# Attention of two layers: output products of two key tiles together, 96-row maxima in three banks, the row of maxima by DMA

## The chip, the cores and the metric

The kernel runs on one core of a Trainium2 chip. The metric is the time of one execution in microseconds (us) on the device. TensorE is called PE, its weight loads PEld, VectorE DVE, ScalarE ACT, GpSimd POOL, SyncE SP.

## The reference

The input is a map of 32 x 32 positions with 384 channels, taken as 1024 tokens. Three parts follow each other.

```python
x = x + conv_attention(group_norm(x))     # layer 0
t = tokens(x)
t = t + attention(layer_norm(t))          # layer 1
t = t + moe(layer_norm(t))                # 8 experts, the best 2 of each token
```

Each attention has 12 heads of 32 columns over the 1024 tokens:

```python
scores = scale * q @ k.T                  # layer 0: + rel_h + rel_w, looked up per row and column
out = softmax(scores, axis=-1) @ v
out = out @ proj_w.T + proj_b
```

In layer 0 the relative positions are added to the scores through a table for rows and one for columns of the map.

## The kernel before, in words

All three parts are one program with hand-written queues for each engine, held together by counting semaphores. `for L in L2` runs each engine through the two attention layers, and the experts follow.

**A layer.** Queries, keys and values are computed (lines 562 and 650). Queries and keys are split into a high and a low part of float32r and stored in DRAM as `heads`, from where SP loads each head's operands: `load_m` (line 366) `qm` and `km` for the maxima, `load_a` (line 374) `qa`, `ka` and in layer 0 `qb` for the scores. Two sets of buffers alternate. `store` (line 385) puts a finished head's quarter rows into `xnT`.

**Maxima.** The softmax needs the maximum of each query's row before the exponential. `max_scores` (line 569) computes, for a tile of 128 queries and a half of the keys, rough scores of the high parts alone in a PSUM bank, in layer 0 with 96 rows (the relative positions too), in layer 1 with 32. The halves alternate between banks 0 and 1. DVE's `maximum` (line 857) reduces each bank of 128 x 512 to a column of `mhalf`, and after the eighth tile `mhalf` to `mcol` (line 864). Head h + 1's last three tiles are treated in steps 0 to 2 of head h, and head h + 2's first five in steps 3 to 7 (`MAXIMA`).

**From a column to a row.** The scores are computed transposed, keys on partitions and queries along the row. So the maxima, one for each query, must become a row. PE transposes `mcol` into bank 7 (`turn_max`, line 578) and ACT copies it in eight pieces into rows 96 to 103 of `qa`, each time with another column of a negated unit matrix (`place_max`, line 1051). Rows 96 to 103 of `ka` are ones, and so the score product subtracts the maximum: it has 104 rows.

**A head.** PE's `head` (line 620) goes through eight key tiles s. Each step has `scores` of tile s (two halves, in layer 0 two products for each, banks 2 to 5 in two pairs), the two maxima products, and `out_product` of tile s - 2 (`BEHIND`). An output product is four `quarters` (line 596): values 128 x 32 are the weights, 256 queries move, and each quarter goes to its own 32 columns of the array and 32 partitions of bank 6. Each fp32 quarter is two records in the trace, so a block of quarters reads "x8". ACT makes the exponential of a tile of 128 x 1024 from two banks into one of five buffers of `prob` (`NP`). The sums of the exponentials come from POOL, which adds the first tiles (`ADDS`: tiles 0 to 5 in layer 0, 0 to 4 in layer 1) into `acc`, and from PE, which multiplies the rest and `acc` with ones (`sums`, line 616). ACT copies both halves of bank 6 to `vsb`, DVE inverts the sums in four pieces (line 870) and multiplies (line 875) into `osb`. DVE also adds the bias of the projection to `t` (line 900) before the last head.

PE's queue fixes the order of its work. A product waits for the buffers and banks that it names; what stands behind it waits too. SP's queue is as strict: `load_m(h + 1)`, `load_a(h)`, in layer 1 three fills with zeros that the experts need, `store(h - 2)`.

## Time and profile before

| | us |
|---|---|
| median of three runs | 1052.12 |
| lowest and highest run | 1039.26, 1052.98 |
| span of the profiled execution | 1051.4 |
| PE busy | 943.1 (90%) |
| DVE busy | 539.0 (51%) |
| ACT busy | 421.2 (40%) |
| POOL busy | 307.3 (29%) |
| heads of layer 0 | from about 122 to 347 |
| heads of layer 1 | from about 431 to 652 |

The profile describes one execution and gives its span, from the first to the last instruction. Its own time is not listed apart from the runs; the span stands 0.7 us below their median. In a row of the timeline stand the start and the duration, engine, line, operation, what is written and read, the count where equal instructions follow each other, and in brackets the idle time before and what ended it. PE's products are pipelined, so a duration is longer than the distance to the next product, and starts are what counts.

### The profile page before, as it was taken

The numbers are of one execution on the slowest core, as the hardware profiler recorded it, in microseconds if no ns is written. First come the engines' busy times: TensorE is split into PE (matmuls) and PEld (weight loads), VectorE is DVE, ScalarE is ACT, GpSimd is POOL, SyncE is SP. The second block draws the span as 40 slices with busy tenths as digits, with TensorE's granted clock in tenths as the row PEclk, the third lists the DMA queues.
The fourth block names the chain that finished last, engine by engine and source line by source line (L and its number), as shares of the span: only waits on it lengthen the run. The fifth ranks groups of instructions, "written<-read, shape, count | busy, mean of one in ns | idle before, by whom it ended". The sixth has DMA issues, their size and how long they took to land.

```text
span 1051.4 us, 17622 instructions
## 1 busy us (share of the span) xinstructions
PE 943.1 (90%) x6029; PEld 625.0 (59%) x6030; DVE 539.0 (51%) x903; ACT 421.2 (40%) x774; POOL 307.3 (29%) x168
## 2 busy tenths in 40 slices
PE   4968899999999899999999999814999999999992
PEld 3456455555554444433444444514999999999992
DVE  4324667676774535534777775560244334433424
ACT  0211265665656222434666766221334323422420
POOL 0000175765758100333565647032000000000203
PEclk9989699999999999756999999856999999999997
DMA  8556523424334039113364556062256246345214
GB/s 280 113 127 175 226 71 98 129 78 120 103 84 147 5 68 233 30 41 106 116 202 127 187 150 207 27 229 79 74 189 232 94 164 229 130 165 192 75 52 135
DMA packets 73951, 139.03 MB, mean 132 GB/s; under 512 B 10800, under 2 KB 48688, under 8 KB 73904
## 3 DMA queue, kind: packets, MB, share of 16 engines
q1 hardware_dynamic: 62736, 120.42, 37.6%
q10 hardware_dynamic: 9120, 11.74, 3.4%
q0 software_dynamic: 2048, 6.29, 1.9%
q8 instruction: 24, 0.39, 0.2%
q14 instruction: 23, 0.19, 0.1%
HBM read 91.29 MB, written 43.45 MB: 128 GB/s over the span
## 4 chain that ended last, share of the span: by engine, by line
PE 72%; DVE 8%; issue 7%; POOL 7%; DMA 3%; ACT 2%; ACTq 1%; SPq 1%; DVEq 0%; POOLq 0%
PE ps L601 13%; PE ps L575 11%; PE ps L591 11%; PE ps L776 10%; PE ps L765 9%; PE ps L562 6%; PE ps L593 4%; POOL qf L501 3%; PE ps L696 2%; PE ps L650 2%; PE ps L672 2%; POOL xs L526 2%; POOL gy L533 2%; DVE w_lo L980 1%; DVE mhalf L860 1%
## 5 line engine op out<-in xcount | busy, mean ns | idle before, releaser
L860 DVE TENSOR_REDUCE mhalf<-ps 128x1 f32<-128x512 f32 x384 | 248.1, 686 | 142.9 <-PE ps L575 138.9
L1043 ACT ACTIVATE prob<-ps 128x1024 f32<-128x1024 f32 x192 | 196.5, 1024 | 146.0 <-PE ps L593 75.3
L501 POOL TENSOR_TENSOR qf<-qf,prob 128x1024 f32<-128x1024 f32 x84 | 205.5, 2447 | 22.3 <-POOL qf L501 9.6
L591 PE MATMUL ps<-qa,ka 104*128 104x512 f32 x384 | 164.4, 470 | 3.6 <-ACT qa L1056 2.9
L765 PE MATMUL ps<-xT,w 128*128 128x128 f32 x1440 | 165.6, 277 | 1.4 <-ACT xT L1114 1.4
L765 PEld LDWEIGHTS ps<-xT,w 128*128 128x128 f32 x1440 | 165.0, 193 | 1.8 <-issue 1.8
L575 PE MATMUL ps<-km,qm 96*128 96x512 f32 (+1 forms) x384 | 150.3, 466 | 4.8 <-DVE mhalf L860 2.8
L601 PE MATMUL ps<-prob,va 128*32 128x256 f32 x1536 | 129.5, 411 | 0.3 <-issue 0.2
L1136 ACT ACTIVATE h_f<-ps,b1c 128x128 f32<-128x128 f32 x240 | 66.9, 378 | 148.8 <-PE ps L765 148.8
L591 PEld LDWEIGHTS ps<-qa,ka 104*128 104x128 f32 x384 | 68.6, 200 | 83.0 <-issue 59.5
L575 PEld LDWEIGHTS ps<-km,qm 96*128 96x128 f32 (+1 forms) x384 | 70.1, 201 | 69.6 <-DVE mhalf L860 42.0
L497 POOL TENSOR_TENSOR qf<-prob 128x1024 f32<-128x1024 f32 x24 | 57.0, 2376 | 163.7 <-ACT prob L1043 163.7
L776 PE MATMUL ps<-w_hi,h_hi 128*128 128x384 f32 x240 | 82.1, 342 | 9.9 <-DVE h_lo L989 9.9
L533 POOL DMA_INDIRECT gy<-low,where_i x8 | 10.0, 1254 | 272.9 <-SPq L471 270.7
L776 PE MATMUL ps<-w_lo,h_hi 128*128 128x384 f32 x240 | 80.4, 335 | 0.0
L776 PE MATMUL ps<-w_hi,h_lo 128*128 128x384 f32 x240 | 80.3, 335 | 0.0
L987 DVE CAST h_hi<-h_f 128x512 fp32r<-128x512 f32 x60 | 25.5, 425 | 103.8 <-ACT h_f L1136 103.8
L593 PE MATMUL ps<-qb,eb 128*128 128x512 f32 x192 | 77.3, 403 | 0.0
L601 PEld LDWEIGHTS ps<-prob,va 128*32 128x32 f32 x1536 | 31.4, 110 | 73.0 <-issue 60.2
L1056 ACT ACTIVATE qa<-ps,negd 8x128 fp32r<-8x128 f32 x192 | 57.7, 349 | 38.4 <-PE ps L581 35.8
L562 PE MATMUL ps<-xnT,wqkv 128*128 128x512 f32 x144 | 64.1, 607 | 3.1 <-DVE xnT L821 3.1
L511 POOL COPY va<-vf 128x256 f32 (+1 forms) x24 | 9.6, 398 | 192.7 <-DVE vf L846 103.3
(129 smaller groups left out, 914.6 us busy)
## 6 DMA issues: line engine op xcount, KB each, us to landing
w<-in_w SPq DMA_DIRECT2D x24, 768.0 KB, 7.4
w_raw<-in_w SPq DMA_DIRECT2D x24, 768.0 KB, 11.9
heads<-parts SPq DMA_DIRECT2D x56, 256.0 KB, 4.6
qa<-heads SPq DMA_DIRECT2D x24, 256.0 KB, 3.8
ka<-heads SPq DMA_DIRECT2D x24, 256.0 KB, 4.3
qb<-heads SPq DMA_DIRECT2D x12, 512.0 KB, 5.3
xs<-zero SPq DMA_DIRECT2D x8, 768.0 KB, 4.9
qm<-heads SPq DMA_DIRECT2D x12, 384.0 KB, 3.7
```

Source lines behind the costliest of these rows:

```text
L501: pool.tensor_tensor(acc[b], acc[b], prob[:, n % NP, :], ALU.add).then_inc(a_ok[L], 1)
L562: last = mm(ps[:, 2 * (u % 2) + half, :], wqkv[:, k, col * P:(col + 1) * P], xnT[:, k, half * HALF:(half + 1) * HALF], start=(k == 0), sto ...
L575: mm(ps[:, half, :], qm[b][0:kr, qt * P:(qt + 1) * P], km[b][0:kr, half * HALF:(half + 1) * HALF], start=True, stop=True).then_inc(sm_ok[L ...
L591: last = mm(out, ka[b][:, s * P:(s + 1) * P], qa[b][:, cols], start=True, stop=(L == 1))
L593: last = mm(out, eb[:, s * P:(s + 1) * P], qb[b][:, cols], start=False, stop=True)
L601: last = mm(ps[HD * r:HD * (r + 1), 6, half * QUARTER:(half + 1) * QUARTER], lhs, src[:, r * QUARTER:(r + 1) * QUARTER], start=start, stop ...
L765: last = mm(ps[:, g, c % HG * P:(c % HG + 1) * P], w1[b][:, k, c * P:(c + 1) * P], xT[:, k, :], start=(k == 0), stop=(k == KT - 1))
L776: last = mm(ps[:, 6, 0:C], h[:, c, :], w[:, c, :], start=(c == 0 and n == 0), stop=(c == HC - 1 and n == 2))
L860: v.tensor_reduce(mhalf[:, b, qt, half:half + 1], ps[:, half, :], AX.X, ALU.max).then_inc(mx_ok[L], 1)
L1043: act.activation(prob[:, s % NP, :], ps[:, 2 + 2 * (s % 2):4 + 2 * (s % 2), :].rearrange("p a b -> p (a b)"), ACT.Exp).then_inc(p_ok[L], 1)
L1056: last = act.activation(qa[b][96:104, i * P:(i + 1) * P], ps[0:TT, 7, 0:P], ACT.Copy, scale=negd[:, i:i + 1])
L1136: last = act.activation(h_f[:, c, :], ps[:, g, c % HG * P:(c % HG + 1) * P], ACT.Relu, bias=b1c[b][:, c:c + 1])
```

## The change

- Order: `head` on PE goes through pairs of key tiles: scores and maxima of both, then the output products of the two tiles of the pair before.
- Maxima: three banks (0 to 2) in a ring written out in `MAX_BANK` and `MAX_BACK`; the scores move to banks 3 to 6, the output to bank 7. The products have 96 rows in layer 1 too; POOL writes zeros into rows 32 to 95 of `qm` once. The tile of queries is now every eighth query (`qt:N:TT`), so that `mcol` read row by row is in the order of the queries.
- Row of maxima: no transposition and no copies by ACT. SP writes `mcol` to DRAM and reads it back as one row into row 96 of `qa` (`load_row`); row 96 of `ka` is -1. The score product has 97 rows.
- POOL multiplies by the inverted sums (`multiply`), after its additions of the next head, and adds the bias of the projection at the layer's start.
- `prob` has six buffers, and in the last head POOL adds only tiles 0 to 2.
- SP's order in the loop is `load_a`, `load_row`, `load_m`, fills, `store`.

```diff
-NP = 5
+NP = 6
...
-BEHIND = 2
 ADDS = (5, 4)
+ADDS_LAST = 2
+MAX_BANK = (0, 1, 2, 0, 1, 2, 0, 1, 2, 0, 1, 2, 0, 1, 2, 1)
+MAX_BACK = (4, 2, 4, 3, 3, 3, 3, 3, 3, 3, 3, 3, 3, 3, 3, 2)
+OUT_BANK = 7
...
+        row_dram = [nc.dram_tensor(f"row{b}", [N], F32).ap() for b in range(2)]
...
+        bd = vsb[:].rearrange("p a b -> p (a b)")[:, 0:2 * REL * 4].rearrange("p (w i g) -> p w i g", w=2, g=4)
...
+                def load_row(h, b):
+                    sp.wait_ge(mc_ok[L], h + 1)
+                    sp.sem_inc(m_free, 1)
+                    sp.dma_start(row_dram[b].rearrange("(p t) -> p t", t=TT), f(mcol[:, b, :])).then_inc(st_row, 16)
+                    wait(sp, st_ok[L], TT * (h - 1))
+                    sp.sem_inc(m_free, 1)
+                    sp.wait_ge(st_row, 16 * (L * NH + 1) + 16 * h)
+                    sp.sem_inc(m_free, 1)
+                    sp.dma_start(f(qa[b][96:97, :]), row_dram[b].unsqueeze(0)).then_inc(ld_row[b], 16)
...
+                load_row(0, 0)
                 load_m(2, 0)
-                load_a(2, 0)
+                load_row(1, 1)
                 load_m(3, 1)
-                store(0, 0, 0)
                 with sp.Fori(0, (NH - 4) // 4) as q:
                     for n in range(4):
-                        h = q * 4 + n + 3
-                        load_m(h + 1, n % 2)
-                        load_a(h, 1 - n % 2)
+                        h = q * 4 + n + 1
+                        load_a(h + 1, n % 2)
+                        load_row(h + 1, n % 2)
...
+                        load_m(h + 3, n % 2)
...
-                        store(h - 2, 1 - n % 2, n + 1, q)
+                        store(h - 1, n % 2, n, q)
+                load_a(NH - 2, 0)
+                load_row(NH - 2, 0)
+                store(NH - 4, 0, NH - 4)
                 load_a(NH - 1, 1)
+                load_row(NH - 1, 1)
...
-                def add_tiles(h, b, last=False):
-                    for n in range(1, ADDS[L] + 1):
+                def add_tiles(h, b, first=False, last=False):
+                    adds = ADDS_LAST if last else ADDS[L]
...
+                    if not first:
+                        multiply(h - 1, 1 - b)
+                def multiply(h, b):
+                    wait(pool, st_o[L][b], 32 * (h - b))
+                    pool.wait_ge(o_rc[L], 4 * (h + 1))
+                    pool.sem_inc(pool_in, 1)
+                    pool.tensor_tensor(osb[b][:], vsb[:, 0, :], rec[:], ALU.mult).then_inc(o_ok[L], 1)
...
+                if L == 0:
+                    pool.wait_ge(ld_c, 16 * 16)
+                    pool.wait_ge(ld_t, 16)
+                else:
+                    pool.wait_ge(sm_ok[0], 2 * TT * NH)
+                    pool.wait_ge(o_ok[0], NH)
+                    pool.sem_inc(pool_in, 1)
+                    for i in L2:
+                        for g in (1, 2):
+                            pool.memset(f(qm[i][g * HD:(g + 1) * HD, :]), 0.0).then_inc(qm_zero, 1)
+                    pool.wait_ge(tn_ok[0], TT)
+                    pool.wait_ge(qm_zero, 4)
+                    pool.sem_inc(pool_in, 1)
+                pool.tensor_tensor(t[:], t[:], bproj[:, L:L + 1, :].broadcast_to([P, TT, C]), ALU.add).then_inc(biased, 1)
                 take_v(0, 0)
-                add_tiles(0, 0)
+                add_tiles(0, 0, first=True)
...
-                kr = 96 if L == 0 else 32
+                kr = 96
                 def max_scores(h, b, qt):
                     if qt == 0:
                         pe.wait_ge(ld_m[L][b], (h - b) * 8 * n_m + 16 * n_m)
                     for half in range(2):
-                        wait(pe, mx_ok[L], 2 * (TT * h + qt) + half - 1)
-                        mm(ps[:, half, :], qm[b][0:kr, qt * P:(qt + 1) * P],
+                        i = 2 * qt + half
+                        wait(pe, mx_ok[L], 2 * TT * h + i - MAX_BACK[i] + 1)
+                        mm(ps[:, MAX_BANK[i], :], qm[b][0:kr, qt:N:TT],
...
                 def scores(h, b, s):
                     if s == 0:
                         pe.wait_ge(ld_a[L][b], (h - b) * 8 * n_a + 16 * n_a)
-                        pe.wait_ge(r_ok[L], h + 1)
+                        pe.wait_ge(ld_row[b], 8 * (h - b) + 8 * L * NH + 16)
                     wait(pe, p_ok[L], TT * h + s - 1)
                     for half in range(2):
-                        out = ps[:, 2 + 2 * (s % 2) + half, :]
+                        out = ps[:, 3 + 2 * (s % 2) + half, :]
                         cols = slice(half * HALF, (half + 1) * HALF)
-                        last = mm(out, ka[b][:, s * P:(s + 1) * P], qa[b][:, cols], start=True, stop=(L == 1))
+                        last = mm(out, ka[b][0:97, s * P:(s + 1) * P], qa[b][0:97, cols], start=True, stop=(L == 1))
...
+                    adds = ADDS[L] if left else ADDS_LAST
+                    for pair in range(TT // 2):
+                        for s in (2 * pair, 2 * pair + 1):
+                            scores(h, b, s)
+                            for later, qt in (MAXIMA_FIRST if first else MAXIMA)[s]:
+                                if left >= later:
+                                    max_scores(h + later, b if later == 2 else 1 - b, qt)
+                        if pair > 0:
+                            for s in (2 * pair - 2, 2 * pair - 1):
+                                out_product(h, b, s, adds)
                         elif not first:
-                            out_product(h - 1, 1 - b, TT + s - BEHIND)
-                        if s == BEHIND - 1 and not first:
-                            sums(h - 1, 1 - b)
-                        if s == TT - AHEAD and left >= 1:
-                            turn_max(h + 1, 1 - b)
+                            for s in (TT - 2, TT - 1):
+                                out_product(h - 1, 1 - b, s, ADDS[L])
+                            sums(h - 1, 1 - b, ADDS[L])
...
-            own(v.memset(bd[:], 0.0))
+            own(v.memset(vsb[:], 0.0))
             for i in L2:
-                v.memset(f(ka[i][96:104, :]), 1.0)
+                v.memset(f(ka[i][96:97, :]), -1.0)
...
-                        v.wait_ge(sm_ok[L], 2 * (TT * h + qt) + half + 1)
-                        v.tensor_reduce(mhalf[:, b, qt, half:half + 1], ps[:, half, :], AX.X, ALU.max).then_inc(mx_ok[L], 1)
+                        i = 2 * qt + half
+                        v.wait_ge(sm_ok[L], 2 * TT * h + i + 1)
+                        v.tensor_reduce(mhalf[:, b, qt, half:half + 1], ps[:, MAX_BANK[i], :], AX.X, ALU.max).then_inc(mx_ok[L], 1)
...
-                        if s == 6 and not first:
-                            output(h - 1, 1 - b)
...
-                if L == 0:
-                    v.wait_ge(ld_t, 16)
-                v.tensor_tensor(t[:], t[:], bproj[:, L:L + 1, :].broadcast_to([P, TT, C]), ALU.add).then_inc(biased, 1)
...
-                        act.activation(prob[:, s % NP, :], ps[:, 2 + 2 * (s % 2):4 + 2 * (s % 2), :].rearrange("p a b -> p (a b)"),
+                        act.activation(prob[:, s % NP, :], ps[:, 3 + 2 * (s % 2):5 + 2 * (s % 2), :].rearrange("p a b -> p (a b)"),
                                        ACT.Exp).then_inc(p_ok[L], 1)
-                        if TT - AHEAD <= s < TT - 1 and not last:
-                            i = s - TT + AHEAD
-                            place_max(h + 1, 1 - b, range(PLACED[i], PLACED[i + 1]))
-                        if s == BEHIND - 1 and not first:
+                        if s == 1 and not first:
                             keep_output(h - 1)
-                def place_max(h, b, tiles):
-                    act.wait_ge(mT_ok[L], h + 1)
-                    wait(act, st_ok[L], TT * (h - 1))
-                    for i in tiles:
-                        last = act.activation(qa[b][96:104, i * P:(i + 1) * P], ps[0:TT, 7, 0:P], ACT.Copy, scale=negd[:, i:i + 1])
-                    if i == TT - 1:
-                        last.then_inc(r_ok[L], 1)
```

The order of PE's instructions in the loop of layer 1, from the third key tile of a head on, was this (va is the head's values, km and qm the operands of the maxima, an ISA or REGISTER row a wait's value).

```order
L591 MATMUL ps<-qa_57,ka_59 128x512 x2
L283 ISA
L575 MATMUL ps<-km_64,qm_62 128x512 x2
L601 MATMUL ps<-prob,va_67 32x256 x4
L283 REGISTER_ALU
L591 MATMUL ps<-qa_57,ka_59 128x512 x2
L572 ISA
L283 REGISTER_ALU
L575 MATMUL ps<-km_63,qm_61 128x512 x2
L601 MATMUL ps<-prob,va_67 32x256 x4
```

Now the same place reads:

```order
L630 MATMUL ps<-qa_57,ka_59 128x512 x2
L286 REGISTER_ALU
L619 MATMUL ps<-km_64,qm_62 128x512
L286 REGISTER_ALU
L619 MATMUL ps<-km_64,qm_62 128x512
L286 REGISTER_ALU
L630 MATMUL ps<-qa_57,ka_59 128x512 x2
L615 ISA
L286 ISA
L619 MATMUL ps<-km_63,qm_61 128x512 x2
L640 MATMUL ps<-prob,va_67 32x256 x8
```

A tile's output product stood behind each maxima pair; now two score and maxima blocks stand together and x8 is two output products.

SP's queue at the start of the loop of layer 1 began with the loads for the maxima (qm, km) and went on to those for the scores (qa, ka).

```order
L371 DMA qm_61<-heads 32x1024
L372 ISA
L372 DMA km_63<-heads 32x1024
L283 ISA
L378 ISA
L378 DMA qa_58<-heads 64x1024
L379 ISA
L379 DMA qa_58<-heads 32x1024
L380 ISA
L380 DMA ka_60<-heads 32x1024
L381 DMA ka_60<-heads 64x1024
```

Now it begins with the loads for the scores, and the row of maxima goes out and comes back before the next load.

```order
L381 DMA qa_57<-heads 64x1024
L382 ISA
L382 DMA qa_57<-heads 32x1024
L383 ISA
L383 DMA ka_59<-heads 32x1024
L384 DMA ka_59<-heads 64x1024
L390 REGISTER_ALU
L392 DMA row<-mcol 128x8
L395 ISA
L397 DMA qa_57<-row 1x1024
L286 REGISTER_ALU
L374 ISA
```

The loads for the maxima moved behind the row, and everything behind `row<-mcol` waits for DVE's `mcol` and for the row's way to DRAM.

## Rows read from the trace of the kernel before

**Rows 1.** TensorE's granted clock in 40 slices of the span, in tenths.

```profile
PEclk9989699999999999756999999856999999999997
```

**Rows 2.** Window of layer 1: us, busy us of PE, PEld, DVE, ACT, POOL, PEclk, DMA.

```profile
435.00:484.00 49.00, 48.94 (x207) 18.01 (x207) 20.74 (x36) 19.40 (x31) 19.16 (x10) 0.50 0.10 24
```

**Rows 3.** Timeline of DVE, first and last `mcol` of heads between which the pace is read.

```profile
148.79 0.17 DVE L864 TENSOR_REDUCE mcol<-mhalf 128x8 f32<-128x16 f32 x1
...
318.98 0.17 DVE L864 TENSOR_REDUCE mcol<-mhalf 128x8 f32<-128x16 f32 x1
...
436.54 0.17 DVE L864 TENSOR_REDUCE mcol<-mhalf 128x8 f32<-128x16 f32 x1
...
495.86 0.17 DVE L864 TENSOR_REDUCE mcol<-mhalf 128x8 f32<-128x16 f32 x1
...
630.66 0.17 DVE L864 TENSOR_REDUCE mcol<-mhalf 128x8 f32<-128x16 f32 x1
```

**Rows 4.** Timeline of PE in layer 0, a head's start and a later key tile.

```profile
201.97 0.61 PE L601 MATMUL ps<-prob,ones 128*32 128x256 f32 x8
...
202.41 0.61 PE L601 MATMUL ps<-qf,ones 128*32 128x256 f32 x8
...
211.65 0.50 PE L591 MATMUL ps<-qa,ka 104*128 104x512 f32 x1
...
212.70 0.62 PE L575 MATMUL ps<-km,qm 96*128 96x512 f32 x2
...
213.24 0.64 PE L601 MATMUL ps<-prob,va 128*32 128x256 f32 x8
...
213.81 0.50 PE L591 MATMUL ps<-qa,ka 104*128 104x512 f32 x1
```

**Rows 5.** Timeline of PE and DVE in layer 1, one key tile at full clock.

```profile
566.38 0.73 PE L591 MATMUL ps<-qa,ka 104*128 104x512 f32 x2
...
566.88 0.54 DVE L870 RECIPROCAL rec<-vsb 128x64 f32<-128x64 f32 x1
...
567.04 0.73 PE L575 MATMUL ps<-km,qm 32*128 32x512 f32 x2
...
567.58 1.29 DVE L860 TENSOR_REDUCE mhalf<-ps 128x1 f32<-128x512 f32 x2
...
567.70 0.64 PE L601 MATMUL ps<-prob,va 128*32 128x256 f32 x8
...
568.26 0.73 PE L591 MATMUL ps<-qa,ka 104*128 104x512 f32 x2
```

**Rows 6.** Timeline of PE, products of 96 columns, moving operand contiguous, then strided.

```profile
58.46 3.71 PE L672 MATMUL ps<-qf,bd 128*128 128x96 f32 x32
...
81.70 6.17 PE L672 MATMUL ps<-qf,bd 128*128 128x96 f32 x36
```

**Rows 7.** Timeline of SP and PE at the first head of layer 0.

```profile
119.53 0.34 SPq L371 DMA_DIRECT2D qm<-heads  x1
...
121.75 0.77 PE L591 MATMUL ps<-qa,ka 104*128 104x512 f32 x1 [2.29 <-ACT qa L1056]
```

**Rows 8.** DMA issues of the page: count, KB each, us to landing.

```profile
ka<-heads SPq DMA_DIRECT2D x24, 256.0 KB, 4.3
...
xnT<-osb SPq DMA_DIRECT2D x92, 32.0 KB, 1.8
```

**Rows 9.** Timeline: PE and POOL in a head, DVE's multiplication, POOL and PE near layer 0's end.

```profile
323.93 5.27 POOL L501 TENSOR_TENSOR qf<-qf,prob 128x1024 f32<-128x1024 f32 x1 [0.18 <-POOL qf L501]
...
346.66 0.64 PE L601 MATMUL ps<-qf,ones 128*32 128x256 f32 x8 [1.36 <-POOL qf L501]
...
555.62 0.73 PE L591 MATMUL ps<-qa,ka 104*128 104x512 f32 x2
...
560.14 2.36 POOL L497 TENSOR_TENSOR qf<-prob 128x1024 f32<-128x1024 f32 x1 [6.29 <-ACT prob L1043]
...
571.24 0.42 DVE L875 TENSOR_TENSOR osb<-vsb,rec 128x256 f32<-128x256 f32 x1
```

More of the change, by code:

```diff
@@ L336, in _ @@
             sp.dma_start(bqk[:], a["bqk"]).then_inc(ld_bq, 16)
-            for dst, name in ((ebf, "eb"), (ident[:], "ident"), (negd[:], "negd"), (before[:], "before")):
+            for dst, name in ((ebf, "eb"), (ident[:], "ident"), (before[:], "before")):
                 sp.dma_start(dst, a[name]).then_inc(ld_c, 16)
@@ L688, in _ @@
                 head(NH - 1, 1, left=0)
-                for s in range(TT - BEHIND, TT):
-                    out_product(NH - 1, 1, s)
-                sums(NH - 1, 1)
+                for s in (TT - 2, TT - 1):
+                    out_product(NH - 1, 1, s, ADDS_LAST)
+                sums(NH - 1, 1, ADDS_LAST)
                 def project(tt, ks):
```

48 lines of the change are left out of this document (16 added, 32 removed).

## The prediction

> **What bounds the kernel now.** The granted clock in 40 slices [rows 1] comes first: TensorE (PE) has full clock almost throughout, with a hole of about 58 us in the second layer's attention. The window from 435 to 484 us [rows 2] shows PE busy for the whole of it at 0.50, that is at 1.2 instead of 2.4 GHz; the same code goes on behind it at 1.00. The start of the small reduction mcol, which runs once a head at its third key tile, gives the pace [rows 3]. Layer 0: (318.98 - 148.79) / 9 = 18.91 us a head. Layer 1 at full clock: (630.66 - 495.86) / 8 = 16.85. Its two heads before that: (495.86 - 436.54) / 2 = 29.66. So the half clock costs 2 x 12.8 = 25.6 us.
>
> Inside a head the timeline shows PE issuing nearly without a break. A key tile of layer 0 takes 213.81 - 211.65 = 2.16 us [rows 4]: four score products up to 212.70 (1.05), two maxima products to 213.24 (0.54), four output quarters to 213.81 (0.57). At a head's start such blocks of quarters follow each other 202.41 - 201.97 = 0.44 apart [rows 4]. A lone block thus costs 0.13 more than one in a row, and the 512-column products around it lose some more: six at about 0.235 are 1.41, the row shows 1.59. Changing between full products and 32-column ones therefore costs 0.13 + 0.18 = 0.31 us a time, and it happens at each of 8 tiles a head.
>
> Layer 1 has two score products and two maxima products a tile, but takes 568.26 - 566.38 = 1.88 us [rows 5], against 4 x 0.235 + 0.44 + 0.31 = 1.69 by the same pieces. The rest is the pair of maxima, 0.66 instead of 0.47: with two banks each product waits for the reduction of the one two before. VectorE is nearly full there, 1.29 for two reductions and 0.54 for a reciprocal [rows 5], and a two-bank ring gives it no lead. PE bounds both layers, VectorE stands just behind in layer 1.
>
> **The change, part by part.** *Pairs.* The change takes 4 of 8 such transitions out of each head: 4 x 0.31 = 1.24 us. A head of layer 0 has 48 products of 512 columns (11.3 us), 11 blocks of quarters (8 of values, 2 of late sums, 1 of the accumulated sum: 4.84) and 4 transitions (1.24): 17.4, and I take 17.5. Layer 1 has 32 products (7.5), 12 blocks (5.3) and 1.24: 14.1.
>
> *What the pairs delay.* The last two output products of a head come behind two score tiles of the next, and with six buffers the first exponential needs the buffer of the seventh tile. In layer 1 that puts exp 0 at 2.1 + 0.9 = 3.1 us from the head's start and its end at 4.2, and PE wants the bank at 4.4. Exp 1 ends at 5.2, PE wants it at 5.35. Hidden, with 0.1 to 0.2 us to spare. In layer 0 exp 0 ends at 5.15 and PE wants it at 5.36. If the cover fails, up to 0.3 us a head is lost, 7 us in all.
>
> *Three banks.* They let a maxima product start while two reductions are outstanding, so the 0.19 a tile in layer 1 goes (8 x 0.19 = 1.5 a head). Late next is VectorE: in the third pair it has four reductions and two reciprocals, about 3.6 us, against PE's 3.1. The bank of the third product behind then stalls PE some 0.5 us. I take 14.7 us for a head of layer 1, between 14.1 (no stall) and 15.6 (0.5 in each of three pairs). VectorE also loses the multiplication of 0.42 [rows 9].
>
> *Steady sum.* Layer 0: 9 heads x (18.91 - 17.5) = -12.7. Layer 1 at full clock: 8 x (16.85 - 14.7) = -17.2.
>
> *Clock.* With 32-row maxima layer 1 had fallen to half clock by 435 us, in its first head, and stayed at 0.50 while PE was busy for all of 49 us [rows 2]; layer 0, whose maxima have 96 rows, keeps full clock once it has it [rows 1]. The change gives layer 1 the 96 rows (two thirds of them zeros on one side). If that keeps the clock, the two slow heads become ordinary: 59.32 - 2 x 14.7 = -29.9, 25.6 of it the clock's and 4.3 the steady gain. If it does nothing, these heads scale as 2 x (14.1 to 14.7), nearly the 29.66 they take, and only about -2 remains. Both ends stay in the range; I take the first, since the one difference between the layers' products that bears on it is removed, and because the clock also held at 32 rows once it was back, so the loss looks marginal. The Trainium skill, "TensorE: Matmul & The Clock Gate" (What's actually happening), says that the gate follows how busy PE has been. Read as time busy this speaks against the gain: PE was 48.94 us busy in 49 at half clock [rows 2], and rows would change nothing; the sum would be the second end. The trace already disagrees with so plain a reading.
>
> *Row of maxima by DMA.* The transposition (one product) and eight ScalarE copies a head go; ScalarE was not the bound, worth 0.1 a head. In their place SP sends 128 x 8 values out and one row of 1024 back, each a transfer at least as long as the smallest here, 1.8 us [rows 8], or as the 4.3 of a load that it queues behind. At the first head of layer 0 the store can only be issued behind the last head stores, where before a load went out at 119.53 [rows 7]; so the row lands at 119.53 + 0.5 + 2 + 0.5 + 2 = 124.5 or a little less, against scores that began at 121.75: +2.3 (bounds +1.5 to +7). At layer 1's first head I add 0.5. In the steady state SP's queue has store of outputs, then load_a, then the row, and stands first behind GpSimd's multiplication, below.
>
> *GpSimd.* Its additions begin at 560.14, when the head's score products began at 555.62 [rows 9]; with exp 1 a microsecond later they begin at 5.4, four additions of 2.36 with gaps and a copy take 11.1, and the multiplication of a quarter of their columns 0.6 to 1.1: it ends 17.5 us from the head's start. Then 2.6 to issue four stores, 2.4 for load_a, 3 to 4 until the row is out (behind loads of 4.3), 2.6 until it is back: 28.1 to 29.1 us, due within two heads, 29.4. The cover is thin: each further microsecond costs half a microsecond a head. In layer 0 it is five additions (multiplication done at 20.4), 2.6, 2.9, 5 and 2.6: 33.5 in 35.0. The bias additions (3072 columns, about three of these, 7 us) lie at the layers' starts, where GpSimd is idle. VectorE's own goes, beside which one GpSimd addition took 5.27 instead of 2.36 at 323.93 [rows 9]; half of those 2.9 us reached PE, as I estimate: -1.5. At the very end of each layer the multiplication moves from 0.42 to about 0.7 on the path: +0.3 twice.
>
> *Two additions in the last head.* PE waited 1.36 us at 346.66 for the last addition [rows 9]. That and the transitions of the last two heads (2 x 1.24) give -3.8 in layer 0, less three more blocks of ones (1.3): -2.5. In layer 1, with two blocks (0.9) and a shorter wait, about -2.0.
>
> *Strided weights.* The maxima's stationary operand is now read with steps of eight values. The only strided fp32 read in the trace is a moving one: 32 products of 96 columns take 3.71 us contiguous (0.116 each), 36 strided 6.17 (0.171) [rows 6]. If a weight load slows as much it takes about 0.2 and hides under a 0.235 product. Bounds: 0 to 0.2 us for each of 384 products, 0 to 77 us; I take 0.01, +4, near the row. "SBUF — State Buffer" of the Trainium skill (The DMA port swizzle) states that fp32 is read at full rate only within 16-byte lines; a step of 32 bytes leaves each, so it expects the slowdown, without a size. The row agrees in kind; the sum would stand, since the size is the row's.
>
> *Sum.* -12.7 - 17.2 - 29.9 - 2.5 - 2.0 - 1.5 + 2.3 + 0.5 + 0.6 + 4 = -58.4, and about -1 for the first heads before their marks: -59.4. The profiled execution's span of 1051.4 gives 992.0. It stands 0.7 under the median of the runs, 1052.12, so 993. The lowest run, 1039.26, shows that something of 13 us varies; half of the clock's 25.6 would be that size.
>
> **Rivals.** *A, the clock stays low in layer 1:* the time is 993 + 26 = 1019. For it: PE was busy and stayed low. Against: layer 0's behaviour.
> *B, the row comes late:* if each of its transfers takes 3 us more (behind the 1.5 MB of zero fills or the loads), the loops are 35 and 39.5 us, the heads 17.5 and 19.75: +2.8 x 10 and +2.25 x 10, about 1044 with the clock kept. Against: 1.8 us for small transfers, and the fills are issued after the row.
> *C, slower:* the strided weight load does not hide. Its place is each of the 384 maxima products; it decides from (59.4 + 4) / 384 = 0.16 us more each, a load of about 0.4 us. At 0.2 it gives 993 - 4 + 77 = 1066. For it: the reads of [rows 6] did slow down. Against: only by half.
> *D, the pairs gain nothing* because the cost of a transition sits elsewhere: the 12.7 of layer 0 and 8 x 1.24 = 9.9 of layer 1 vanish, 1016. The 0.44 and 0.57 of [rows 4] speak against.
>
> **How the numbers follow.** Forecast 0.62, A 0.18, B 0.08, C 0.04, D 0.08. The range reaches from 978 (14.1 us a head in layer 1, a free strided read) over A and D to 1028. A measurement of this kernel can tell about 2% from no change, 21 us. Faster by over 2% is the forecast, A, D and half of B, 0.92; same 0.04; slower 0.04, C.
>
> **What would show it.** Right: mcol every 17.5 us in layer 0 and 14.7 in layer 1; granted clock 1.0 through layer 1; maxima products 0.235 apart; two blocks of quarters 0.44 apart and one transition per pair; 4 exponentials in 8 waiting for PE alone. Wrong: PE's score products waiting for the row's DMA, maxima products waiting for VectorE in each pair, 0.50 around 430 to 490, or weight loads of the maxima over 0.23 us.

## The result and the profile after

The changed kernel takes 997.8 us (median of four runs, 992.37 to 999.31); the kernel before, on the same chip, 1052.4 (four runs, 1039.26 to 1052.98). The ratio is 0.9486, with an interval of 0.9428 to 0.9544: faster, 5 us above the forecast of 993 and inside its range. The profiled execution took 997.88, with a span of 996.1 against 1051.4. The kernel before varies much more than the changed one: in 27 later executions it took 1029.91 to 1070.83 us, with a mean granted clock from 0.910 to 0.948. The ratios use only the executions of a kernel within 1.5% of its quickest (fast ones), which leaves out slow ones of before, so they can stand nearer to 1 than the medians do.

Cut at the first score product of each layer (rows L591 before, L630 after) and at the first product of the projection, the 55.3 us of span come from these places:

| stretch | before | after | difference |
|---|---|---|---|
| to layer 0's first scores | 121.8 | 123.5 | +1.7 |
| attention of layer 0 | 225.4 | 209.8 | -15.6 |
| from there to layer 1's scores | 83.7 | 83.5 | -0.2 |
| attention of layer 1 | 221.0 | 181.0 | -40.0 |
| the rest | 399.5 | 398.3 | -1.2 |

The granted clock of the changed kernel in 40 slices, answering to [rows 1]:

```profile
PEclk9989699999999999999999999559999999999996
```

The hole of [rows 1] in the 17th to 19th slice is gone; the one further on lies behind the attention of layer 1 and stands in both. Two windows of layer 1 (busy us of PE, PEld, DVE, ACT, POOL, then PEclk), answering to [rows 2]:

```profile
414.00:470.00 56.00, 52.74 (x421) 34.71 (x419) 40.92 (x73) 29.09 (x32) 34.03 (x20) 1.00 0.40 119
470.00:583.00 113.00, 110.41 (x947) 71.34 (x944) 83.34 (x150) 60.86 (x67) 77.69 (x45) 1.00 0.52 158
```

PE is now a little less busy than in [rows 2] (94 and 98% of the time instead of all of it) and has the full clock throughout. The timeline of DVE, `mcol` once a head, answers to [rows 3]:

```profile
148.43 0.17 DVE L905 TENSOR_REDUCE mcol<-mhalf 128x8 fp32r<-128x16 f32 x1
...
308.49 0.17 DVE L905 TENSOR_REDUCE mcol<-mhalf 128x8 fp32r<-128x16 f32 x1
...
437.32 0.17 DVE L905 TENSOR_REDUCE mcol<-mhalf 128x8 fp32r<-128x16 f32 x1
...
562.25 0.17 DVE L905 TENSOR_REDUCE mcol<-mhalf 128x8 fp32r<-128x16 f32 x1
```

Layer 0: (308.49 - 148.43) / 9 = 17.78 us a head instead of 18.91. Layer 1: (562.25 - 437.32) / 8 = 15.62 instead of 16.85, and no head of 29.66. A pair of layer 0 on PE, answering to [rows 4]:

```profile
221.14 0.50 PE L630 MATMUL ps<-qa,ka 97*128 97x512 f32 x1
...
222.20 0.64 PE L619 MATMUL ps<-km,qm 96*128 96x512 f32 x2
222.67 0.39 PE L630 MATMUL ps<-qa,ka 97*128 97x512 f32 x1
...
225.19 0.50 PE L630 MATMUL ps<-qa,ka 97*128 97x512 f32 x1
```

The pair takes 225.19 - 221.14 = 4.05 us. Two tiles of [rows 4] took 4.32. The two maxima products stand 0.47 apart as a couple (222.20 to 222.67), so a product still takes 0.235 beside its strided weights. Layer 1, PE from the first pair of a head to the third, answering to [rows 5]:

```profile
508.37 0.74 PE L630 MATMUL ps<-qa,ka 97*128 97x512 f32 x2
...
512.98 0.74 PE L630 MATMUL ps<-qa,ka 97*128 97x512 f32 x2
...
514.52 0.40 PE L619 MATMUL ps<-km,qm 96*128 96x512 f32 x1
...
515.34 0.63 PE L619 MATMUL ps<-km,qm 96*128 96x512 f32 x1 [0.43 <-DVE mhalf L901]
...
515.90 1.07 PE L640 MATMUL ps<-prob,va 128*32 128x256 f32 x16
...
516.90 0.74 PE L630 MATMUL ps<-qa,ka 97*128 97x512 f32 x2
...
518.43 0.87 PE L619 MATMUL ps<-km,qm 96*128 96x512 f32 x2
...
519.23 1.07 PE L640 MATMUL ps<-prob,va 128*32 128x256 f32 x16
520.23 0.74 PE L630 MATMUL ps<-qa,ka 97*128 97x512 f32 x2
```

The four pairs of such a head take 4.61, 3.92, 3.33 and 3.75. Without any wait they would take 4.39, 3.07, 3.07 and 3.51 by the pieces of the prediction (0.235 for a product, 0.44 for a block of quarters, 0.31 for the change between them). The row of 515.34 shows the largest loss: one maxima product waits 0.43 us for a reduction, in ten heads of the layer. The rest is small and in every pair: the last couple of maxima products takes 518.43 to 519.23, 0.80 instead of the 0.57 that such a couple takes in layer 0 (223.62 to 224.19).

### The profile page after: what moved, and what is told of

Same layout as the page of the kernel before. It is cut to its first block, busy times and chain, and to the rows that moved or that the text cites. A ratio compares the mean times of both kernels' runs of the same rounds, so it can differ in the third digit from the quotient of the medians.

```text
span 996.1 us, 17661 instructions
## 1 busy us (share of the span) xinstructions
PE 879.5 (88%) x6045; PEld 675.1 (68%) x6046; DVE 500.9 (50%) x879; ACT 353.8 (36%) x582; POOL 322.3 (32%) x191
## 4 chain that ended last, share of the span: by engine, by line
PE 41%; issue 7%; DVE 6%; POOL 4%; DMA 4%; SPq 4%; ACT 1%; ACTq 1%; DVEq 0%; POOLq 0%
PE ps L816 11%; PE ps L805 9%; PE ps L640 6%; PE ps L630 5%; PE ps L619 5%; SPq L362 2%; PE ps L736 2%; POOL xs L569 2%; POOL gy L576 2%; DVE w_lo L1016 1%; DMA xnT<-osb 1%; PE ps L605 1%; DVE mhalf L901 1%; POOL qf L521 1%; DMA heads<-parts 1%
## 5 line engine op out<-in xcount | busy, mean ns | idle before, releaser
L1079 ACT ACTIVATE prob<-ps 128x1024 f32<-128x1024 f32 x192 | 190.4, 1026 | 219.5 <-PE ps L640 95.7
L521 POOL TENSOR_TENSOR qf<-qf,prob 128x1024 f32<-128x1024 f32 x79 | 188.2, 2383 | 16.2 <-POOL qf L521 8.6
L619 PE MATMUL ps<-km,qm 96*128 96x512 f32 x384 | 149.1, 463 | 7.8 <-DVE mhalf L901 6.8
L630 PE MATMUL ps<-qa,ka 97*128 97x512 f32 x384 | 146.8, 425 | 8.6 <-DMA qa<-row 8.6
L619 PEld LDWEIGHTS ps<-km,qm 96*128 96x128 f32 x384 | 113.3, 320 | 36.1 <-DVE mhalf L901 21.1
L640 PE MATMUL ps<-prob,va 128*32 128x256 f32 x1536 | 107.5, 385 | 0.0
L630 PEld LDWEIGHTS ps<-qa,ka 97*128 97x128 f32 x384 | 69.4, 191 | 54.5 <-issue 27.9
L911 DVE RECIPROCAL rec<-vsb 128x64 f32<-128x64 f32 x96 | 49.8, 535 | 39.0 <-ACT vsb L1087 39.0
L640 PEld LDWEIGHTS ps<-prob,va 128*32 128x32 f32 x1536 | 40.3, 109 | 41.2 <-issue 24.0
L1029 DVE TENSOR_TENSOR ysb<-ps,b2c 128x384 f32<-128x384 f32 x20 | 11.1, 557 | 90.7 <-PE ps L816 90.7
```

The source lines that it names most:

```text
L521: pool.tensor_tensor(acc[b], acc[b], prob[:, n % NP, :], ALU.add).then_inc(a_ok[L], 1)
L619: mm(ps[:, MAX_BANK[i], :], qm[b][0:kr, qt:N:TT], km[b][0:kr, half * HALF:(half + 1) * HALF], start=True, stop=True).then_inc(sm_ok[L], 1)
L630: last = mm(out, ka[b][0:97, s * P:(s + 1) * P], qa[b][0:97, cols], start=True, stop=(L == 1))
L640: last = mm(ps[HD * r:HD * (r + 1), OUT_BANK, half * QUARTER:(half + 1) * QUARTER], lhs, src[:, r * QUARTER:(r + 1) * QUARTER], start=star ...
L1079: act.activation(prob[:, s % NP, :], ps[:, 3 + 2 * (s % 2):5 + 2 * (s % 2), :].rearrange("p a b -> p (a b)"), ACT.Exp).then_inc(p_ok[L], 1)
```

## The experiments

**Rows of the maxima products.** The forecast laid the clock to the 32 rows and the 1.88-us tile to the two banks. *e1* takes the kernel before and gives it the 96 rows alone:

```diff
-                kr = 96 if L == 0 else 32
+                kr = 96
```

together with GpSimd's zeros in rows 32 to 95 of `qm` from the change.

> The kernel before with one thing of the change: the maxima products of layer 1 have 96 rows (rows 32 to 95 zeros in qm). Theory (the rows keep the clock): granted clock 1.0 through the heads of layer 1, the marks mcol of its first heads 16.9 us apart instead of 30.1 and 29.2, time 1052 - 25 = 1027. Rival (the clock depends on how long TensorE is busy, or was kept by the pairs or the banks): still about 58 us at 0.50, time 1052, the same.

It took 1013.5 us (1012.65 to 1017.82), a ratio of 0.9806 [0.968, 0.9931] to its kernel before. Between the profiled executions attention of layer 1 went from 221.0 to 184.7 us, and the span by 39.5; against the two quickest executions of before measured beside it (1029.91 and 1039.46) e1 is only 20 us faster. The granted clock by slices shows no hole at the 18th:

```profile
PEclk9979699999999999999999999658999999999996
```

And a window of its layer 1, columns as above, has PE nearly as busy as [rows 2]:

```profile
420.00:500.00 80.00, 79.12 (x591) 39.51 (x589) 63.61 (x107) 53.89 (x87) 44.98 (x24) 1.00 0.41 119
```

So with the rows alone this execution keeps its clock. The other executions agree: their mean granted clock is 0.947 to 0.954 in e1's four, and 0.910 to 0.948 in the seven of before measured beside them. The rows did something unforeseen too: heads at full clock went from 16.86 to 15.8 with two banks still, about 11 us in all, and therefore e1 is faster than the 1027 expected. The weight loads (PEld) say why. First the kernel before, the tile of [rows 5] and VectorE's reductions ahead of it:

```profile
566.37 0.30 PEld L591 LDWEIGHTS ps<-qa,ka 104*128 104x128 f32 x2 [0.41 <-issue]
567.04 0.29 PEld L575 LDWEIGHTS ps<-km,qm 32*128 32x128 f32 x2 [0.37 <-DVE mhalf L860]
```

```profile
565.68 1.29 DVE L860 TENSOR_REDUCE mhalf<-ps 128x1 f32<-128x512 f32 x2 [0.15 <-PE ps L575]
```

Then e1, the loads of one tile, and the products of the same:

```profile
560.12 0.30 PEld L601 LDWEIGHTS ps<-qa,ka 104*128 104x128 f32 x2 [0.41 <-issue]
560.47 0.48 PEld L585 LDWEIGHTS ps<-km,qm 96*128 96x128 f32 x2
```

```profile
560.12 0.74 PE L601 MATMUL ps<-qa,ka 104*128 104x512 f32 x2
560.70 0.63 PE L585 MATMUL ps<-km,qm 96*128 96x512 f32 x2
561.27 0.64 PE L611 MATMUL ps<-prob,va 128*32 128x256 f32 x8
```

With 32 rows the first load of the maxima comes 0.67 us after that of the scores and with its product (567.04 for both); with 96 rows it comes 0.35 after it, under the running score product, and the maxima product follows 0.58 after the first score product instead of 0.66. The same happens once more on the way out of the couple (0.57 instead of 0.66). A change between 104 and 32 rows thus costs about 0.09 us each time, and there are two in a tile: that was the 0.19. The brackets of the load at 567.04 name VectorE's `mhalf` as what it waited for, as the prediction thought. But the bank of this first product is that of the first of the two reductions from 565.68 on, which was over about 0.7 us earlier, and the next experiment leaves only the rows as a difference.

*e9* is e1 with `kr = 96 if L == 0 else 64`.

> The kernel before with 64 rows in layer 1's maxima (e1 had 96). Two things came with 96 rows: the clock stayed at 1.0 and a key tile took 1.70 instead of 1.89 us, because the weights of the first maxima product were loaded under the score product before it. If the tile's loss belongs to 32-row weights beside 104-row ones (another cut of the array), 64 rows may keep it or not: kept means 1.89, gone means 1.70. If the clock follows the rows used, 64 rows lie between: 0.50 for less than 58 us or not at all, time 1013 to 1035. If it needs all 96, 1040 to 1053.

It has e1's zeros and e1's wait for them. It took 1036.25 (ten runs, 1029.44 to 1053.35), a ratio of 0.9958 [0.9917, 0.9999]: about no gain. Its heads at full clock are 16.87, as in before. The weight load of its maxima on PEld is late as in before, and a window of its layer 1 has the clock partly down:

```profile
568.76 0.30 PEld L585 LDWEIGHTS ps<-km,qm 64*128 64x128 f32 x2 [0.36 <-DVE mhalf L872]
```

```profile
425.00:465.00 40.00, 39.87 (x167) 15.53 (x166) 18.68 (x31) 16.07 (x26) 12.98 (x8) 0.66 0.12 32
```

So neither the zeros nor the wait made e1's pace or its clock. The hole lasted 27.3 us here against 58.0 in the profile of before. One profile can't tell whether that is the rows or chance: the kernel before ran between 1029.9 and 1070.8, and e9's own runs spread by 24. In the cost of the change 64 rows act as 32 do. *e2* is the counter-test, the changed kernel with 32 rows in layer 1:

```diff
-                kr = 96
+                kr = 96 if L == 0 else 32
```

> The changed kernel with 32 rows again in layer 1's maxima. Theory (rows keep the clock): 0.50 comes back at the first head of layer 1 for some 50 us, time 998 + 20 to 26 = 1018 to 1024. Rival (pairs and banks keep the clock busy enough): clock stays 1.0, 998, the same.

It took 1063.97 (1051.94 to 1076.47), a ratio of 1.021 [0.9935, 1.0486]: the whole gain is gone, and 66 us over the changed kernel. The mean granted clock of its executions is 0.891 to 0.918, that of the changed kernel's 0.945 to 0.951. Its granted clock by slices, and a window of layer 1:

```profile
PEclk9989599999999999569696969855999999999996
```

```profile
425.00:450.00 25.00, 25.00 (x122) 10.30 (x121) 9.02 (x14) 5.94 (x7) 7.05 (x3) 0.50 0.16 43
```

The clock falls again and again, mostly in stretches of 17 to 27 us, while PE is busy all the time. Heads take 17.6 to 28.9 us, and about 17.6 at full clock, more than the 16.86 of before. The pairs don't help there: a pair has as many changes of row count as two single tiles.

**Pairs and banks.** *e3* goes back to single tiles in `head` and keeps the rest:

```diff
-                    for pair in range(TT // 2):
-                        for s in (2 * pair, 2 * pair + 1):
...
+                    for s in range(TT):
...
+                        if s >= 2:
+                            out_product(h, b, s - 2, adds)
```

> The changed kernel with TensorE's order of before: one output product behind each key tile. Theory (each change between full and 32-column products costs 0.31 us, four more a head): heads of layer 0 17.78 + 1.24 = 19.0 us, layer 1 15.60 + 0.6 to 1.2 (part of it lies under VectorE's waits), time 998 + 24 to 29 = 1022 to 1027. Rival (the gain of layer 0 came from the transposition and ScalarE's copies that went): heads of layer 0 17.8 to 18.0, time 998 to 1003.

It took 1010.79 (1007.79 to 1020.63), a ratio of 0.9751 [0.9638, 0.9864]. Heads of layer 0 are 18.83 again, +1.05 over 17.78; heads of layer 1 at full clock are 15.69, only +0.09 where 0.6 to 1.2 was expected. So the pairs are worth 13 us, nearly all in layer 0, and the three banks, the row by DMA and GpSimd's multiplication bring nothing there in the single order: most heads of before took 18.8 too.

The profiled execution of e3 shows one thing more, a window of its layer 1:

```profile
430.00:450.00 20.00, 20.00 (x84) 9.43 (x83) 9.75 (x17) 7.24 (x8) 9.83 (x5) 0.50 0.12 34
```

This kernel has 96 rows and was at half clock for 20.5 us all the same. In the 5 us before, PE had been busy for 3.56, with one wait of 1.44 us for the row of maxima. The changed kernel has the same wait there, 3.43 us busy in 415 to 420, and kept its clock. e3's four other executions took 1007.79 to 1010.8 with a mean granted clock of 0.949 to 0.953, against 1020.63 and 0.939 for this one. So 96 rows make the fall rarer and shorter; they don't rule it out.

*e6* keeps the pairs and has two banks:

```diff
-MAX_BANK = (0, 1, 2, 0, 1, 2, 0, 1, 2, 0, 1, 2, 0, 1, 2, 1)
-MAX_BACK = (4, 2, 4, 3, 3, 3, 3, 3, 3, 3, 3, 3, 3, 3, 3, 2)
+MAX_BANK = (0, 1, 0, 1, 0, 1, 0, 1, 0, 1, 0, 1, 0, 1, 0, 1)
+MAX_BACK = (2, 2, 2, 2, 2, 2, 2, 2, 2, 2, 2, 2, 2, 2, 2, 2)
```

> The changed kernel with its maxima in two banks in turn (bank 2 idle). Theory (with pairs four maxima products come within 1.2 us and the ring of banks holds them; each waits 0.7 us of reduction after the one two before): the second maxima block of each pair waits some 0.3 to 0.6 us, heads of layer 1 15.60 + 1 to 2 = 16.6 to 17.6, layer 0 17.78 + 0 to 0.8, time 998 + 11 to 26 = 1009 to 1024. Rival (three banks are worth nothing, as in the single order): 998, the same.

It took 1028.2 (1027.55 to 1030.47), a ratio of 0.9874 [0.979, 0.9958]. A pair of its layer 1 on PE:

```profile
503.69 0.74 PE L630 MATMUL ps<-qa,ka 97*128 97x512 f32 x2
504.27 0.65 PE L619 MATMUL ps<-km,qm 96*128 96x512 f32 x2
...
505.46 1.22 PE L619 MATMUL ps<-km,qm 96*128 96x512 f32 x2
506.61 1.07 PE L640 MATMUL ps<-prob,va 128*32 128x256 f32 x16
507.61 0.74 PE L630 MATMUL ps<-qa,ka 97*128 97x512 f32 x2
```

The second couple takes 505.46 to 506.61, 1.15 us instead of 0.80, and starts 0.24 late; a pair takes 3.92. Heads: 18.85 and 17.42, in layer 0 more than the forecast allowed. With four maxima products in quick succession the later ones wait for a whole reduction. The third bank is worth 30 us with pairs. Without it the pairs bring nothing in layer 0 (18.85) and cost 1.6 us a head in layer 1 (17.42 against 15.8 in e1, which has single tiles and two banks, but also the old way of the row). It is what the pairs need; a gain of its own in the single order is not shown.

*e4* only moves the two places where the ring of three is broken, since 16 is not a multiple of 3:

```diff
-MAX_BANK = (0, 1, 2, 0, 1, 2, 0, 1, 2, 0, 1, 2, 0, 1, 2, 1)
-MAX_BACK = (4, 2, 4, 3, 3, 3, 3, 3, 3, 3, 3, 3, 3, 3, 3, 2)
+MAX_BANK = (0, 1, 2, 0, 1, 2, 1, 0, 2, 1, 0, 2, 1, 0, 1, 2)
+MAX_BACK = (3, 3, 3, 3, 3, 3, 2, 4, 3, 3, 3, 3, 3, 3, 2, 4)
```

> The changed kernel with another table of banks: the two places where the ring of three breaks (a bank used again after one product) are the first products of the second and the fourth pair (products 14 and 6) instead of the second of tile 7 and of tile 0 (products 15 and 1). Theory (the second pair of each head, 3.92 us in layer 1 and 4.38 in layer 0, is long because product 1 waits for the reduction of product 15): layer 0 17.78 - 0.34 = 17.4, layer 1 15.60 - 0.6 = 15.0, time 998 - 10 = 988. Rival (VectorE is the bound, the wait moves to the next pair): same pace in layer 1, time 994 to 998.

It took 986.58 (982.87 to 988.04), a ratio of 0.9523 [0.9403, 0.9643]. The pair that contained the row of 515.34 is now 3.32:

```profile
502.01 0.74 PE L630 MATMUL ps<-qa,ka 97*128 97x512 f32 x2
...
503.54 0.85 PE L619 MATMUL ps<-km,qm 96*128 96x512 f32 x2
...
505.33 0.74 PE L630 MATMUL ps<-qa,ka 97*128 97x512 f32 x2
```

Heads: 17.44 (-0.34) and 15.02 (-0.60), 11 us in all with the ends of the layers. A product that may look back only two places waits for the reduction of the product two before it, which in a burst has only just begun. That is harmless where it opens a pair, right behind output products, as 6 and 14 do; in the changed kernel it was 15 and 1, the second and the last of one pair.

**Weights and transport.** *e5* reads the maxima's weights contiguously and has SP write the row one value at a time to put it in order:

```diff
-                        mm(ps[:, MAX_BANK[i], :], qm[b][0:kr, qt:N:TT],
+                        mm(ps[:, MAX_BANK[i], :], qm[b][0:kr, qt * P:(qt + 1) * P],
...
-                    sp.dma_start(row_dram[b].rearrange("(p t) -> p t", t=TT), f(mcol[:, b, :])).then_inc(st_row, 16)
+                    sp.dma_start(row_dram[b].rearrange("(t p) -> p t", p=P), f(mcol[:, b, :]), allow_slow_non_contiguous=True).then_inc(st_row, 16)
```

> The changed kernel with the maxima's weights read contiguously (a tile is 128 neighbouring queries again); so that the row still comes in order, SP writes mcol to DRAM one value at a time. Theory (the strided weight load takes 0.32 instead of 0.19 us but hides under the product before it): weight loads at 0.19, products of one pair still 0.235 to 0.245 apart, heads of layer 0 within 0.1 of 17.78 unless the row comes late. Rival (the stride costs time): spacing 0.235 against 0.245 at every one of 16 products plus the first one, heads 0.3 to 1 us shorter.

One run took 1159.47, against 1040.84 for before beside it. The group of the maxima's weight loads in the changed kernel (partitions x elements, count, busy us, mean ns, waits), then in e5:

```profile
L619 PEld LDWEIGHTS ps<-km,qm 96*128 96x128 f32 x384 | 113.3, 320 | 36.1 <-DVE mhalf L901 21.1 <-ACT prob L1057 1.1 <-issue 1.0
```

```profile
L619 PEld LDWEIGHTS ps<-km,qm 96*128 96x128 f32 x384 | 86.0, 225 | 52.8 <-DVE mhalf L901 30.5 <-ACT prob L1057 1.1 <-issue 1.1
```

And a line of e5's waits (us in total, times, longest):

```profile
PE ps L630 <- DMA qa<-row: 95.0, 18, 16.8
```

A contiguous load takes 0.19 (the mean of 225 includes stretches at half clock), a strided one 0.32. Under a running product both hide. Behind a wait for VectorE the load can't be early, and the difference shows: the pair of layer 1 that takes 3.33 in the changed kernel takes 3.18 in e5, and one of layer 0 0.02 to 0.04 less. With 44 pairs in each layer that is 44 x 0.15 + 44 x 0.04: an estimate of about 8 us for the stride, from a single profiled execution. Both forecasts were half right: the load hides in layer 0 and does not in layer 1. The last line is the other result: written value by value, the row comes late 18 times, most heads take 21 to 24 us, and at each such wait the clock falls to half, mostly for 6.8 us. The changed kernel's line of waits, and its transfers of `row`:

```profile
PE ps L630 <- DMA qa<-row: 8.6, 2, 7.1
```

```profile
DMA to landing us min/median/max: 1.5/3.1/5.3
```

Two waits in all, at the first head of each layer; 22 rows are hidden.

**The first row.** In layer 0 PE waits 7.12 us for it in the changed kernel:

```profile
120.49 0.35 SPq L392 DMA_DIRECT2D row<-mcol  x1
...
122.02 0.30 SPq L397 DMA_DIRECT2D qa<-row  x1
...
123.49 0.77 PE L630 MATMUL ps<-qa,ka 97*128 97x512 f32 x1 [7.12 <-DMA qa<-row]
```

*e7* puts `load_row(0, 0)` of both layers ahead of SP's wait for the last stores of heads, and *e8* joins that with e4's ring.

> The changed kernel with one thing moved in SP's queue: the first head's row of maxima is sent out and back before SP waits for the last head stores of the layer, not behind them. Theory (the first score product of each layer waits for that row, 7.1 us in layer 0 and 1.4 us in layer 1): layer 0 begins 2 to 5 us earlier, layer 1 1 us, time 998 - 3 to 6 = 992 to 995. Rival (the row then queues behind the stores in the DMA queue and lands no earlier): the same, 998.

> The bank table of e4 and the early row of e7 together. If both causes are what they seem and lie at different places, the gains add: 986.6 - 3 to 6 = 981 to 984, faster than both kernels. If the early row only moves the wait, 986 to 987.

e7 took 996.56 (993.54 to 997.4; ratio 0.9558 [0.9475, 0.9642]), e8 984.28 (984.06 to 985.71; ratio 0.9449 [0.9369, 0.9529]): 1 and 2 us under the kernels without it, which these runs can't tell from nothing. In e7 the row of layer 0 leaves 8.7 us sooner, but it is read back only 0.5 sooner:

```profile
111.77 0.35 SPq L392 DMA_DIRECT2D row<-mcol  x1
121.48 0.30 SPq L397 DMA_DIRECT2D qa<-row  x1
```

From one issue to the other it takes 9.7 us behind the stores of the heads, and 1.5 in the changed kernel, where SP had waited for these. *e10* (with e4's ring) issues both transfers of the first row from ScalarE:

```diff
-                load_row(0, 0)
+                if L == 1:
+                    load_row(0, 0)
...
+                if L == 0:
+                    act.wait_ge(mc_ok[0], 1)
+                    act.dma_start(row_dram[0].rearrange("(p t) -> p t", t=TT), f(mcol[:, 0, :])).then_inc(st_row, 16)
+                    act.wait_ge(st_row, 16)
+                    act.dma_start(f(qa[0][96:97, :]), row_dram[0].unsqueeze(0)).then_inc(ld_row[0], 16)
```

> e4 (the new bank table) with the first head's row of layer 0 moved by ScalarE's DMA queue instead of SP's, as soon as the column is there. Theory (the row waited behind the head stores in SP's queue, on the wire as well, and TensorE 6 to 7 us for it): the first score product at 117 to 119 instead of 122.5 us, time 986.6 - 3 to 5 = 982 to 984. Rival (the DMA engines are full with the stores, the queue does not matter): 122, 986.

It took 983.54 (981.52 to 985.87), a ratio of 0.9408 [0.9309, 0.9507].

```profile
111.35 0.35 ACTq L1096 DMA_DIRECT2D row<-mcol  x1
116.72 0.49 ACTq L1098 DMA_DIRECT2D qa<-row  x1
119.20 0.76 PE L631 MATMUL ps<-qa,ka 97*128 97x512 f32 x1 [2.42 <-DMA qa<-row]
```

In its own queue the row takes 5.4 us where e7's took 9.7, and the scores begin 3.3 us sooner than in e4. The median is 3 us below e4's 986.58, but the two sets of runs overlap. *e12* is e10 with layer 1's first row ahead of SP's wait for stores too.

> e10 with layer 1's first row too sent before SP waits for the last stores of queries and keys. Layer 1's first score product waited 1.4 us for it. If e10's gain holds, this adds about 1: 981 to 983; the best of all. If not, as e8: 984.

It took 983.17 (981.45 to 984.49), a ratio of 0.9406 [0.9309, 0.9504]: the same as e10. Its row in layer 1 leaves 1.1 us sooner than in e10 (402.83 for 403.96) and is read back 0.9 later (406.76 for 405.82). Both take 14 us less than the changed kernel and 58 less than the median of before measured beside them, 1041.47. That median stood at 1052.4 in the first measurement; the 11 us between the two are before's own variation.

**Who multiplies.** *e11* gives the multiplication back to VectorE:

```diff
-                    if not first:
-                        multiply(h - 1, 1 - b)
...
+                        if s == 6 and not first:
+                            output(h - 1, 1 - b)
```

> The changed kernel with the multiplication by the inverted sums back on VectorE (0.4 to 0.8 us a head), at the end of its seventh step. If VectorE were the bound of layer 1, heads grow by 0.4 to 0.8 (16.0 to 16.4), time 1002 to 1008. If TensorE waits only for the ring of banks, at fixed places of the pair, heads stay at 15.6 to 15.8, 998 to 1001.

It took 1010.61 (1007.36 to 1011.15), a ratio of 0.9664 [0.9563, 0.9765]. That is beyond both forecasts. Layer 0 keeps its 17.79; heads of layer 1 go from 15.60 to 16.8, and two of them to 18.5 and 18.6, in which the clock fell for 3.4 us, again with 96 rows. GpSimd, DVE and PE of its layer 1:

```profile
511.20 2.37 POOL L521 TENSOR_TENSOR qf<-qf,prob 128x1024 f32<-128x1024 f32 x1 [0.18 <-POOL qf L521]
...
511.77 2.09 DVE L914 TENSOR_TENSOR osb<-vsb,rec 128x256 f32<-128x256 f32 x1
513.78 2.47 DVE L899 TENSOR_REDUCE mhalf<-ps 128x1 f32<-128x512 f32 x4
...
549.84 0.62 PE L617 MATMUL ps<-km,qm 96*128 96x512 f32 x1 [0.79 <-DVE mhalf L899]
```

The multiplication, 0.42 in [rows 9], takes 2.09 and ends 0.29 after GpSimd's addition. In layer 0 it falls between two additions and takes 0.43 to 0.55. The reductions behind it come late, and PE waits. The Trainium skill, "SBUF — State Buffer" (SBUF: two separate sides), says that a VectorE operation with two inputs in SBUF and one of GpSimd that reads SBUF hold the same ports by turns, each for its whole length. These rows agree.

## Why the prediction was right, and where it was not

*Clock: right.* The two slow heads were to save 29.9 and saved 59.32 - 2 x 15.62 = 28.1. e1, e2 and e9 show the cause from both sides: 96 rows alone keep the clock in the kernel before and 64 don't, 32 rows alone lose it in the changed kernel. Rival A is out. (By the prediction's own clock paragraph, with only 2 us left of this term, it stood at 1021 and not at 1019.) Two limits remain. e3 and e11 lost the clock for 20.5 and twice 3.4 us with 96 rows (and e5 behind its long waits). And the 28.1 belong to the profiled execution of before with its hole of 58 us: the change saved 55 us of span against that one, while before's quickest execution, 1029.91 with a mean granted clock of 0.948, stands only 32 above the changed kernel. Of the plain reading of the Trainium skill, "TensorE: Matmul & The Clock Gate" (What's actually happening), by which time busy decides, e1's window (79.12 of 80 us at 1.00) and e2's (25.00 of 25 at 0.50) leave nothing: PE is busy all the time in both.

*Pairs: right in layer 0, given back in layer 1.* The ordinary pair of layer 0 takes 4.03 to 4.05 against 4.01 by the prediction's pieces, and e3 measures 1.05 a head of the 1.24. The head is 17.78 and not 17.5 because of the breaks of the ring, 0.34 by e4, which the prediction did not look at: -10.1 instead of -12.7. In layer 1 the 1.24 did not come: single tiles cost only 0.09 more there (e3), since the pairs run into the waits for VectorE described below; with e4's ring the pairs stand 0.67 below e3 (15.02 against 15.69). Rival D is out for layer 0.

*The step that failed inside a forecast that held* is "with two banks each product waits for the reduction of the one two before ... so the 0.19 a tile in layer 1 goes". It does go, but e1 removes it with two banks: it belonged to the 32 rows. Half of it sat in the two score products, which take 0.66 us in [rows 5] and 0.58 in e1 and wait for no bank of the maxima. The third bank was what the pairs needed (e6). With that the prediction's account of layer 1 loses its footing: it credited the banks with a gain that they don't give. Its head of 14.7 took 14.1 and one stall of 0.5 in the third pair. Measured are 14.1 + 4 x 0.24 for the last couple of every pair, in which product and strided load wait for a reduction, + 0.60 for the breaks: 15.66, against 15.62. So the term of layer 1 came to 8 x (16.85 - 15.62) = -9.9 instead of -17.2. The bound of 15.6 had been named; the value chosen below it was the error, and it was mostly made good by what follows.

*Strided weights.* +4 was taken; e5 gives about 8 by estimate, and it is part of the 0.24, not beside it. The sign that was to show it wrong, loads above 0.23, came (0.32), and still rival C is far off: a longer load costs only where nothing runs above it.

*Row of maxima: right.* First scores at 123.49 against "124.5 or a little less", +1.7 for +2.3. Layer 1's start moved by -0.2 for +0.5. In the steady state the estimate was 28.1 to 29.1 us from the start of a head to the landing. In the timeline, a head that starts at 508.37 has its additions from 514.09 (5.7, predicted 5.4) and its multiplication at 524.87 (ends at 17.2, predicted 17.5), the row leaves at 531.29 and is read back from 534.17 on, 25.8 us after the start. A transfer of the row lands 1.5 to 5.3 us behind its issue, so this one is there after 27 to 31 us, and two heads take 31.2, not 29.4: the cover is as thin as was said, and the slower heads helped it. Rival B's transport is not there, but e5 shows that its mechanism is: with it, 95 us of waits.

*GpSimd.* VectorE's bias additions went; what they gave is not separated. "+0.3 twice" never came, as the last multiplication of each layer stays on VectorE. The prediction gave the multiplication itself almost nothing, 0.42 off VectorE. That was its length in layer 1; in nine heads of layer 0 it took 1.04 to 1.73 in before. e11 shows that in the new order it is worth 13 us, since on VectorE it would lie behind an addition of GpSimd.

*The sum.* Short by 2.6 (layer 0's pace), 7.3 (layer 1's) and 1.8 (slow heads), 11.7 in all. Back come the +4 that these paces already hold, 0.6 for the multiplications, 1.3 for both first rows, and 1.7 that is left over and lies in the layers' ends and behind them: 4.1, which is 59.4 against 55.3. The forecast was near in part by luck, because errors cancelled. The range's lower end of 978 is 5 us below what the two terms named for it give, 993 - 6 - 4 = 983.

Open: why the clock of PE falls with 32 rows and hardly with 96 of which 64 are zeros, and what set it off in e3; how the hole of before is spread over its executions, of which only the mean clocks (0.910 to 0.948, and 0.926 for the profiled one with 58 us) are known; what the bias additions and six buffers bring by themselves, which was not tried.

## What to carry to other kernels

Before laying a gap between two products to the buffers behind them, compare the shapes on either side: here products of 104 and 96 rows follow each other smoothly, of 104 and 32 or 64 not, and with the smaller shape the clock fell far more often. Padding with zero rows was the larger part of the gain: 39.5 of 55.3 us of span between the profiled executions, and 20 us against the quickest of before. When an order makes bursts of products, count the buffers for a burst and put any break of a ring at its opening, not at its end: two rewritten tables of numbers were worth 11 us.

## What the runs showed of the hardware

- A change between products of 104 rows and of 32 or 64 costs about 0.09 us each time; the weights are not loaded under the product before (0.67 us behind the load before them), and with 96 rows they are (0.35).
- PE was busy for all of 25 us at half clock with 32-row maxima (e2), and for 79.12 of 80 at full clock with 96-row ones (e1). With 96 rows it was also at half clock for 20.5 us, behind a wait of 1.44 us (e3).
- A weight load with steps of eight fp32 values takes 0.32 us instead of 0.19. It hides under a product of 512 columns; where the product ahead waits for a reduction, a pair takes 0.15 more.
- A transfer of 4 KB took 9.7 us from its issue to the issue behind it where large stores were under way in its queue, 5.4 from another queue beside the same stores, 1.5 behind them.
- VectorE's two-input operation of 0.42 us takes 2.09 beside a GpSimd addition of 2.37; the reductions are not slowed by one (two in 1.29 at 514.00 in the changed kernel, beside an addition from 514.09 to 516.47).
